# Cosine weights of four states on VectorE alone, Pool folding in three steps, gathers spread, another order of the drain

## The chip, the cores and the metric

The kernel runs as one program on one core of a Trainium2 chip. The metric is the device time of one execution in microseconds; three runs were made.

## What is computed

A recommendation tower over 1024 tokens. Two encoders (real and imaginary) turn the input into four states of 512 complex values for each token; attention over the four states, with 8 heads, follows; then the interference of the states, a measurement, and a small network. The interference is what the change is about:

```
R = attn_r @ int_Wr[n] - attn_i @ int_Wi[n]        # for each state n of 4
I = attn_r @ int_Wi[n] + attn_i @ int_Wr[n]
f = cos(angle between state i and state j) * strength[i, j]
sup_r = sum over i, j of f * R_j ;  sup_i = the same with I_j
sup   = sup / norm(sup)
mr, mi = sup times meas_Mr, meas_Mi ; amp = sqrt(mr^2 + mi^2)
out   = gelu(layernorm(amp @ post_W.T + post_b)) ; then three layers of the top network
```

The strengths, 16 for each token, are gathered from four embedding tables by index. In the kernel the cosine is the product of unit vectors (state divided by its magnitude), and a state of length zero counts as one with cosine 1.

## The kernel before

Three phases come one after the other: the first layers and the second layers of the encoders, up to about 1600 us, and `phase_states`, in which all of the change lies. There every engine has its own in-order list of instructions, written out by hand; semaphores tie the lists together, and there is no planner. Matrix products are done as three fp32r products of high and low parts (`split3`, lines 50 to 52).

**Attention.** 16 blocks of 64 tokens (`BT`). For each block TensorE projects queries and keys (`project`), scores (`score`), makes values (`values`), and for the block before it turns the softmax weights (`t_turn`, bank `pm`), mixes (`mix`) and projects out (`project_out`). ACT copies the turned weights (`pt_evac`), makes the high part of the mix (`o_high`) and of the output (`t_high`); VectorE spreads the weights (`spread`) and makes the low parts (`o_low`, `t_low`). SP loads block b+1 (`load_s`) when values of block b are done, and stores the output (`store_a`). After the loop the last block is drained by lists written out for each engine, among which weight pieces of the next stage are split (`pieces`). `o_high` of a block writes the buffer that `project_out` of the block before it reads, so it waits for that (`wo_full`). Pool issues 32 gathers for all eight token tiles in one go as soon as the indices are there.

**Interference.** 8 tiles of 128 tokens; the loops of the engines run over t. For each tile:
- SP loads the turned attention output of state n into one of two buffers (`load`); ACT negates a part (`negate`).
- TensorE: `vectors(t, n)`, 48 matmuls into banks 2n and 2n+1, for n = 0 to 3. It waits until the unit vector of tile t-1 has read the banks.
- ACT: `squares` (into `mag` and `sqi`), and after the sum, `magnitude` (a flag for zero, and the square root); for states 2 and 3 also `seed`, a reciprocal square root that VectorE refines.
- Pool: `add_squares`, the sum of two squares; `cosine` of pair (0, 1), two products and an addition into `pc` (`HELPED`); and `fold` of the tile before: states 0, 1 are added to 2, 3 (line 865), then those two to the sum `sup` (line 869). Its order is sums 0, 1, 2, both folds of t-1, sum 3, cosine.
- VectorE: `units` (reciprocal and unit vector for states 0 and 1, lines 1357 and 1370), `refine` (lines 1361 and 1363), unit vectors 2 and 3, then the six pairs: product (line 1382), inner addition (1383), addition of the zero flags (1384), and weighings (1393) into `inv`; `rescale` (1405); and at the end `product` (line 1443), the states times their weights, which signals `weighed`.
- ACT: `begin`, the first weight of each state, after the pairs (0, j); `length` and `scale` for the tile before.

Unit vector n of tile t+1 writes into `cs`, which the fold of tile t reads, so it waits for `folded`.

**Tail.** The last tile is written out; between its pairs lie the first stages of a pipeline over 8 tiles (turn, measure, amplitude, post, top layers), in which TensorE has about 20 us of work for each tile.

Of the kernel before, what the change touches and what calls it, by code (L numbers as in the profile page):

```python
# [9 lines left out]
ACT = mybir.ActivationFunctionType  # L10
# [486 lines left out]
def phase_states(nc, g):  # L497
# [13 lines left out]
    HELPED = [(0, 1)]  # L511
    WEIGHED = {(0, 1): 0, (0, 2): 1, (0, 3): 1, (1, 2): 2, (1, 3): 2, (2, 3): 2}
    TAKES = sum(WEIGHED[p] for p in HELPED)
    STEPS = 2 + 1 + 6 + 2 * (6 - len(HELPED)) + 3 + sum(WEIGHED.values()) - TAKES
    W_MR, W_MI, W_POST, W_T1, W_T2 = 0, KD, 2 * KD, 3 * KD, 4 * KD
    with s.ctx:
# [48 lines left out]
        pc = s.sb("pc", [P, 2, W])  # L565
# [69 lines left out]
        helped = s.sem("helped")  # L635
        taken = s.sem("taken")
# [87 lines left out]
        def p_of(i, j):  # L724
            return pc[:, 0, :] if (i, j) in HELPED else tt[:, 0, :]

        @block.sync
        def _(sp):
# [126 lines left out]
        @block.gpsimd  # L855
        def _(pool):
            def add_squares(t, n):
                pool.wait_ge(squared, t * 8 + (2 * n + 2))
                pool.tensor_tensor(sqi[:, n % 2, :], mag[:, n, :], sqi[:, n % 2, :], ALU.add).then_inc(summed, 1)

            def fold(t, i):

                if i == 0:
                    pool.wait_ge(weighed, t + 1)
                    pool.tensor_tensor(cs[:, :, 2:4, :], cs[:, :, 0:2, :], cs[:, :, 2:4, :], ALU.add).then_inc(folded, 1)
                else:
                    pool.wait_ge(folded, t * 2 + 1)
                    pool.wait_ge(stored, t * 16)
                    pool.tensor_tensor(sup[:, :, :], cs[:, :, 2, :], cs[:, :, 3, :], ALU.add).then_inc(folded, 1)

            def cosine(t, i, j):
                x = HELPED.index((i, j))
                pool.wait_ge(unit, done_units(t, j))

                if (i, j) == (0, 1):
                    if not zeroth(t):
                        if TAKES:
                            pool.wait_ge(taken, t * TAKES)
                        pool.wait_ge(w_begun, t * N)
                elif (i, j) == (0, 2):  # L880
                    pool.wait_ge(w_begun, t * N + 2)
                else:
                    pool.wait_ge(taken, t * TAKES + 1)
                    pool.wait_ge(w_begun, t * N + 3)
                for part in range(2):
                    pool.tensor_tensor(pc[:, part, :], cs[:, part, i, :], cs[:, part, j, :], ALU.mult).then_inc(helped, 1)
                pool.wait_ge(helped, t * (3 * len(HELPED)) + (3 * x + 2))
                pool.tensor_tensor(pc[:, 0, :], pc[:, 0, :], pc[:, 1, :], ALU.add).then_inc(helped, 1)

            def body(t, first):  # L890
                add_squares(t, 0)
                add_squares(t, 1)
                add_squares(t, 2)
                if not first:
                    fold(t - 1, 0)
                    fold(t - 1, 1)
                add_squares(t, 3)
                for i, j in HELPED:
                    cosine(t, i, j)
# [9 lines left out]
            body(0, True)  # L909
            body(1, False)  # L910
            with pool.Fori(2, TT) as t:
                body(t, False)
            fold(LAST, 0)
            fold(LAST, 1)

        @block.scalar
        def _(act):
# [104 lines left out]
            def squares(t, n):  # L1022
                act.wait_ge(multiplied, t * 8 + (2 * n + 2))
                if not zeroth(t):
                    act.wait_ge(rescaled, t * 3 - (2 - min(n, 2)))
                act.activation(mag[:, n, :], g.ps[:, 2 * n, :], ACT.Square).then_inc(squared, 1)
                if n >= 2:
                    act.wait_ge(mag_done, t * N + (n - 1))
# [4 lines left out]
            def magnitude(t, n):  # L1033
                act.wait_ge(summed, t * N + (n + 1))
                act.activation(zero[:, n, :], sqi[:, n % 2, :], ACT.Relu, scale=-1.0 / LEAST, bias=k01[:, 1:2])
                act.activation(mag[:, n, :], sqi[:, n % 2, :], ACT.Sqrt, bias=k01[:, 0:1]).then_inc(mag_done, 1)

            def seed(t):
                act.wait_ge(mag_done, t * N + N)
# [18 lines left out]
            def length(t):  # L1058
                act.wait_ge(folded, t * 2 + 2)
# [13 lines left out]
            def body(t, first):  # L1073
                squares(t, 0)
                magnitude(t, 0)
                negate(t, 3)
                squares(t, 1)
                magnitude(t, 1)
# [74 lines left out]
            t_high(LAST_B - 1, 3)  # L1153
            o_high(LAST_B, 1)
            pt_evac(LAST_B, 2)
            o_high(LAST_B, 2)
            pt_evac(LAST_B, 3)
# [19 lines left out]
            magnitude(t, 0)  # L1177
            negate(t, 3)
            squares(t, 1)
            magnitude(t, 1)  # L1180
            pieces(2 * NP, 2 * NP + KD)
            squares(t, 2)
            magnitude(t, 2)
# [3 lines left out]
            magnitude(t, 3)  # L1187
# [36 lines left out]
        def _(dve):  # L1224
# [118 lines left out]
            class Tile:  # L1343
                def __init__(self, t, first):
                    self.t, self.first, self.done, self.takes = t, first, 0, 0
# [7 lines left out]
                def invert(self, n):  # L1353
                    dve.wait_ge(mag_done, self.t * N + (n + 1))
# [3 lines left out]

                def refine(self):
                    dve.wait_ge(seeded, self.t + 1)  # L1360
                    self.link(dve.scalar_tensor_tensor(out=tt[:, :, :], in0=mag[:, 2:4, :], scalar=-1.0, in1=sqi[:, :, :],
                                                       op0=ALU.mult, op1=ALU.mult))
                    dve.scalar_tensor_tensor(out=inv[:, 2:4, :], in0=tt[:, :, :], scalar=2.0, in1=sqi[:, :, :],
# [3 lines left out]
                def unit_vector(self, n):  # L1367
                    if not self.first and n % 2 == 0:
                        dve.wait_ge(folded, self.t * 2 - (1 - n // 2))
# [3 lines left out]
                def pair(self, i, j):  # L1373
                    t, p = self.t, p_of(i, j)
                    self.link(dve.tensor_tensor(zz[:, :], zero[:, i, :], zero[:, j, :], ALU.add))
                    if (i, j) in HELPED:
                        dve.wait_ge(helped, t * (3 * len(HELPED)) + 3 * (HELPED.index((i, j)) + 1))
                    else:
                        dve.wait_ge(unit, done_units(t, j))
                        if (i, j) != (0, 2):  # L1380
                            dve.wait_ge(w_begun, t * N + (3 if i == 0 else 4))
                        self.link(dve.tensor_tensor(tt[:, :, :], cs[:, :, i, :], cs[:, :, j, :], ALU.mult))  # L1382
                        self.link(dve.tensor_tensor(p, p, tt[:, 1, :], ALU.add))  # L1383
# [7 lines left out]
                def weigh(self, i, j, a, b):  # L1391
                    dve.wait_ge(st_in, self.t + 1)
                    ins = dve.scalar_tensor_tensor(out=inv[:, b, :], in0=p_of(i, j),  # L1393
                                                   scalar=st[:, a * N + b:a * N + b + 1],
                                                   in1=inv[:, b, :], op0=ALU.mult, op1=ALU.add)
                    if (i, j) in HELPED:
                        ins.then_inc(taken, 1)
                        self.takes += 1
                        dve.wait_ge(taken, self.t * TAKES + self.takes)
                    else:  # L1400
                        self.link(ins)
# [39 lines left out]
                def product(self):  # L1441
# [3 lines left out]
                    assert self.done == STEPS and self.takes == TAKES  # L1445

            def body(t, first):
                tile = Tile(t, first)
                tile.units()
# [100 lines left out]
            sup_low(0)  # L1550
            tile.refine()
            tile.unit_vector(2)
            tile.unit_vector(3)
            tile.pair(0, 1)
# [37 lines left out]
        def _(pe):  # L1592
# [124 lines left out]
            project_out(LAST_B - 1, 2)  # L1717
            mix(LAST_B, 0)
            t_turn(LAST_B, 1)
# [236 lines left out]
```

## Time and profile before

| what | value |
|---|---|
| three runs | 3201.33, 3205.56, 3205.1 us; median 3205.1 |
| profiled execution | 3230.8 us, span 3229.1 us |
| TensorE busy | 3002.5 us (93%) |
| VectorE busy | 1566.5 us (49%) |
| ACT busy | 1118.1 us (35%) |
| Pool busy | 311.4 us (10%) |

The busy shares are means over stages of very different kind. In most of the first half of the span VectorE is busy for two tenths or less; in the interference stage, from about 2615 to 3060 us, for about eight. The profiled execution is one execution; the medians come from runs without a profile.

### The profile page before, as it was taken

The page shows a single profiled execution, that of the slowest core. Times are in us where ns is not written, and L with a number is a line of the kernel's source. Part 1 is how long each engine was busy: PE and PEld are TensorE (multiplying, and loading weights), DVE is VectorE, ACT ScalarE, POOL GpSimd, SP SyncE. Part 2 cuts the span into 40 slices and gives each one's busy share as a digit, 9 for nine tenths or more (in the row PEclk, how much of TensorE's full clock was granted, in tenths as well). Part 3 has the DMA queues.
Part 4 walks back from the last instruction along what each step waited for, and adds up shares of the span by engine and source line. Part 5 has one row for each costly group of instructions (what it writes and reads, how often), then busy time and mean ns, then how long its engine had stood idle before and what let it go on. Part 6 is the DMA issues. An engine that isn't in the chain of part 4 may idle for free. (4 is left out here: it accounts for less than half of the span.)

```text
span 3229.1 us, 43945 instructions
## 1 busy us (share of the span) xinstructions
PE 3002.5 (93%) x15808; PEld 2578.3 (80%) x15808; DVE 1566.5 (49%) x2779; ACT 1118.1 (35%) x1889; POOL 311.4 (10%) x289
## 2 busy tenths in 40 slices
PE   7999999999699999999759999999999989898798
PEld 6888888888588877888658999999999977676686
DVE  3222222221621216111156766767667658888873
ACT  3111111110421115111135555545545555454454
POOL 1000000000111101011130000000000003324200
PEclk9999999999899999999979999999999999999899
DMA  5222222221533325233332232231231374444410
GB/s 193 75 71 75 75 71 75 73 64 38 179 118 101 97 66 169 76 97 101 109 101 66 53 91 65 65 91 52 77 79 52 98 176 90 93 91 84 117 62 11
DMA packets 364352, 285.48 MB, mean 88 GB/s; under 512 B 280192, under 2 KB 280320, under 8 KB 364160
## 3 DMA queue, kind: packets, MB, share of 16 engines
q1 hardware_dynamic: 341632, 206.97, 24.0%
q0 software_dynamic: 22656, 77.67, 6.9%
q8 instruction: 38, 0.62, 0.1%
q14 instruction: 26, 0.21, 0.0%
HBM read 194.40 MB, written 90.18 MB: 88 GB/s over the span
## 5 line engine op out<-in xcount | busy, mean ns | idle before, releaser
L50 PE MATMUL banks<-a_whi,a_xhi 128*128 128x512 f32 x1152 | 450.1, 391 | 24.2 <-DVE a_wlo L179 17.7
L52 PE MATMUL banks<-a_whi,a_xlo 128*128 128x512 f32 x1152 | 449.0, 390 | 0.0
L51 PE MATMUL banks<-a_wlo,a_xhi 128*128 128x512 f32 x1152 | 448.9, 390 | 0.0
L50 PE MATMUL banks<-b_ghi,b_whi 128*128 128x512 f32 x1024 | 401.9, 392 | 10.0 <-DVE b_slo L389 8.8
L52 PE MATMUL banks<-b_ghi,b_wlo 128*128 128x512 f32 x1024 | 398.9, 390 | 0.0
L51 PE MATMUL banks<-b_glo,b_whi 128*128 128x512 f32 x1024 | 398.8, 389 | 0.0
L179 DVE TENSOR_TENSOR a_wlo<-a_wraw,a_whi 128x512 fp32r<-128x512 f32 x144 | 99.6, 691 | 577.3 <-ACT a_whi L165 577.3
L50 PE MATMUL banks<-t_sx,s_whi 128*128 128x256 f32 x1024 | 293.3, 286 | 58.4 <-DVE s_wlo L1309 24.1
L165 ACT ACTIVATE a_whi<-a_wraw 128x512 fp32r<-128x512 f32 x144 | 91.3, 634 | 667.2 <-PE banks L52 628.4
L374 DVE TENSOR_TENSOR b_wlo<-b_wraw,b_whi 128x512 fp32r<-128x512 f32 x128 | 88.2, 690 | 445.0 <-ACT b_whi L326 444.8
L52 PE MATMUL banks<-t_sx,s_wlo 128*128 128x256 f32 x1024 | 290.0, 283 | 0.0
L51 PE MATMUL banks<-t_sx,s_whi 128*128 128x256 f32 x1024 | 289.7, 283 | 0.0
L50 PEld LDWEIGHTS banks<-a_whi,a_xhi 128*128 128x128 f32 x1152 | 216.8, 188 | 72.2 <-issue 17.7
L1231 DVE TENSOR_SCALAR t_ks<-banks,cols 64x256 f32<-64x256 f32 x512 | 236.3, 481 | 63.3 <-PE banks L52 56.1
L52 PEld LDWEIGHTS banks<-a_whi,a_xlo 128*128 128x128 f32 x1152 | 216.7, 188 | 45.2
L51 PEld LDWEIGHTS banks<-a_wlo,a_xhi 128*128 128x128 f32 x1152 | 216.8, 188 | 44.9
L50 PE MATMUL banks<-s_whi,s_axng 128*128 128x512 f32 x512 | 209.2, 409 | 36.9 <-DVE s_cs L1370 34.0
L50 PEld LDWEIGHTS banks<-t_sx,s_whi 128*128 128x128 f32 x1024 | 195.8, 191 | 59.8 <-DVE s_wlo L1309 24.8
L326 ACT ACTIVATE b_whi<-b_wraw 128x512 fp32r<-128x512 f32 x128 | 80.5, 631 | 458.1 <-PE banks L52 457.3
L50 PEld LDWEIGHTS banks<-b_ghi,b_whi 128*128 128x128 f32 x1024 | 192.7, 188 | 54.9 <-DVE b_slo L389 13.3
L52 PEld LDWEIGHTS banks<-b_ghi,b_wlo 128*128 128x128 f32 x1024 | 192.4, 188 | 40.2
L51 PEld LDWEIGHTS banks<-b_glo,b_whi 128*128 128x128 f32 x1024 | 192.7, 188 | 39.2
(159 smaller groups left out, 5641.2 us busy)
## 6 DMA issues: line engine op xcount, KB each, us to landing
a_wraw<-w_first SPq DMA_DIRECT2D x144, 256.0 KB, 2.6
b_wraw<-w_second SPq DMA_DIRECT2D x128, 256.0 KB, 2.6
t_sx<-s_scr SPq DMA_DIRECT2D x64, 512.0 KB, 4.6
a_scr<-t_at SPq DMA_DIRECT2D x256, 128.0 KB, 2.1
s_axng<-a_scr SPq DMA_DIRECT2D x64, 512.0 KB, 6.0
s_wraw<-w_pieces SPq DMA_DIRECT2D x82, 256.0 KB, 4.6
h_scr<-a_hst POOLq DMA_DIRECT2D x72, 256.0 KB, 2.7
b_hl<-h_scr POOLq DMA_DIRECT2D x16, 1024.0 KB, 5.9
```

What stands on the lines that cost most here:

```text
L50: mm(out, ahi, bhi, start=first, stop=False)
L51: mm(out, ahi, blo, start=False, stop=False)
L52: return mm(out, alo, bhi, start=False, stop=last)
L165: act.activation(whi[:, k % SPL, :], wraw[:, k % RAW, :], ACT.Copy).then_inc(w_hi, 1)
L179: dve.tensor_tensor(wlo[:, k % SPL, :], wraw[:, k % RAW, :], whi[:, k % SPL, :].bitcast(F32), ALU.subtract).then_inc(w_split, 1)
L326: act.activation(whi[:, j % SPL, :, :].rearrange("p a n -> p (a n)"), wraw[:, j % RAW, :], ACT.Copy).then_inc(w_hi, 1)
L374: dve.tensor_tensor(wlo[:, j % SPL, :, :].rearrange("p a n -> p (a n)"), wraw[:, j % RAW, :], whi[:, j % SPL, :, :].bitcast(F32).rearrange ...
L1231: ins = dve.tensor_scalar(ks[half(at_half), m % 2, h, part, :], b_k[half(h), m % 2, e * C:(e + 1) * C], bcol(M_K + e, m, half(h)), float(s ...
```

## The change

- **Pool** no longer adds squares and no longer makes a cosine. It only folds, in three steps: state 0 to 2, state 1 to 3, and then those two to `sup`. A unit vector waits for the step that reads its state.
- **VectorE** adds the squares: those of states 2 and 3 in one instruction over 1024 elements (`add_23`, between unit vector 0 and reciprocal 1), those of states 0 and 1 of the next tile (`add_squares`) after pairs (1,2) and (2,3). It makes pair (0,1) whole, which now comes before `refine`.
- **ACT** squares into a buffer `sqr` of its own instead of `mag`, and takes the magnitudes of states 2 and 3 in one go. It no longer has to wait for `rescaled` before it squares, but before it takes a magnitude.
- **Gathers**: those of tile t wait for `projected` of block t+2, so that four are issued in each of the blocks 2 to 9.
- **Drain of the last block**: TensorE turns the weights of m+1 before it mixes m; ACT's `pt_evac` and VectorE's `spread` move ahead of `o_high` and `o_low`.
- **SP**: `load(0, 2)` moves ahead of the last eight weight pieces of the stage.
- **Last tile**: `pair(0, 1)` moves ahead of `refine` there too, behind `pieces` and `sup_low(0)`.

```diff
@@ sync
             for i in range(NP + 4 * KD, NP + 6 * KD):
                 piece(i)
+            load(0, 2)
             sp.wait_ge(wo_full, LAST_B * 4 + 4)
             for i in range(NP + 6 * KD, 2 * NP):
                 piece(i)
-            load(0, 2)
             load(0, 3)
@@ gpsimd
-            def add_squares(t, n):
-                pool.wait_ge(squared, t * 8 + (2 * n + 2))
-                pool.tensor_tensor(sqi[:, n % 2, :], mag[:, n, :], sqi[:, n % 2, :], ALU.add).then_inc(summed, 1)
...
+            def fold(t):
+                pool.wait_ge(weighed, t + 1)
+                for n in range(2):
+                    pool.tensor_tensor(cs[:, :, n + 2, :], cs[:, :, n, :], cs[:, :, n + 2, :], ALU.add).then_inc(folded, 1)
+                pool.wait_ge(folded, t * 3 + 2)
+                pool.wait_ge(stored, t * 16)
+                pool.tensor_tensor(sup[:, :, :], cs[:, :, 2, :], cs[:, :, 3, :], ALU.add).then_inc(folded, 1)
             for t in range(TT):
+                pool.wait_ge(projected, (t + 2) * 8 + 5)
                 for f, tbl in enumerate((g.tbl_0, g.tbl_1, g.tbl_2, g.tbl_3)):
...
@@ scalar
             def squares(t, n):
                 act.wait_ge(multiplied, t * 8 + (2 * n + 2))
-                if not zeroth(t):
-                    act.wait_ge(rescaled, t * 3 - (2 - min(n, 2)))
-                act.activation(mag[:, n, :], g.ps[:, 2 * n, :], ACT.Square).then_inc(squared, 1)
...
+                act.activation(sqr[:, n % 2, :], g.ps[:, 2 * n, :], ACT.Square).then_inc(squared, 1)
...
                 squares(t, 2)
-                magnitude(t, 2)
                 squares(t, 3)
-                magnitude(t, 3)
+                magnitude(t, 2, 4)
                 seed(t)
@@ scalar, drain of the last block
+            pt_evac(LAST_B, 1)
             o_high(LAST_B, 0)
-            pt_evac(LAST_B, 1)
...
@@ vector
+                def add_23(self):
+                    dve.wait_ge(squared, self.t * 8 + 8)
+                    dve.tensor_tensor(sqi[:, :, :], sqr[:, :, :], sqi[:, :, :], ALU.add).then_inc(summed, 1)
...
                 def units(self):
                     self.invert(0)
                     self.unit_vector(0)
+                    self.add_23()
                     self.invert(1)
                     self.unit_vector(1)
...
                 tile.units()
+                tile.pair(0, 1)
                 tile.refine()
                 tile.unit_vector(2)
                 tile.unit_vector(3)
-                tile.pair(0, 1)
                 tile.pairs_02()
...
                 tile.pairs_12()
+                add_squares(t + 1, 0)
                 tile.pairs_13()
                 tile.pairs_23()
+                add_squares(t + 1, 1)
                 tile.product()
@@ vector, drain of the last block
+            spread(LAST_B, 2)
             o_low(LAST_B, 0)
-            spread(LAST_B, 2)
             pieces(NP + 2, NP + 4)
             t_low(LAST_B - 1, 3)
+            spread(LAST_B, 3)
             o_low(LAST_B, 1)
-            spread(LAST_B, 3)
@@ tensor, drain of the last block
             project_out(LAST_B - 1, 2)
+            t_turn(LAST_B, 1)
             mix(LAST_B, 0)
-            t_turn(LAST_B, 1)
             project_out(LAST_B - 1, 3)
+            t_turn(LAST_B, 2)
             mix(LAST_B, 1)
-            t_turn(LAST_B, 2)
+            t_turn(LAST_B, 3)
             mix(LAST_B, 2)
-            t_turn(LAST_B, 3)
             mix(LAST_B, 3)
```

## Rows read from the trace of the kernel before

**Rows 1.** Windows: stretch, length, busy us of each engine, TensorE's granted clock, DMA.

```profile
2655.00:2707.00 52.00, 52.00 (x224) 41.84 (x223) 36.95 (x40) 24.44 (x37) 9.57 (x7) 1.00 0.51 100
2812.00:2865.00 53.00, 47.52 (x196) 37.84 (x196) 46.97 (x44) 26.74 (x41) 17.26 (x9) 0.94 0.44 89
```

**Rows 2.** Waits, 2330 to 3229 us: waiting <- releaser, us, times, longest.

```profile
PE banks L50 <- DVE s_cs L1370: 34.0, 6, 6.1
...
DVE s_tt L1361 <- ACT s_sqi L1040: 24.8, 7, 13.9
```

**Rows 3.** Timeline of TensorE and ACT: start, duration, instruction, idle before.

```profile
2641.38 0.50 PE L50 MATMUL banks<-s_whi,s_axng 128*128 128x512 f32 x1 [2.92 <-DMA s_axng<-a_scr]
...
2820.49 0.79 PE L50 MATMUL banks<-s_whi,s_axng 128*128 128x512 f32 x1 [5.49 <-DVE s_cs L1370]
...
2825.62 1.16 ACT L1040 ACTIVATE s_sqi<-s_sqi,s_k 128x1024 f32<-128x1024 f32 x1
...
2863.17 1.16 ACT L1019 ACTIVATE s_axng<-s_axng 128x512 fp32r<-128x512 f32 x2 [4.26 <-DMA s_axng<-a_scr]
```

**Rows 4.** Timeline of VectorE, interference stage.

```profile
2703.52 4.43 DVE L1443 TENSOR_TENSOR s_cs<-s_cs,s_inv 128x4096 f32<-128x4096 f32 x1
...
2809.14 4.42 DVE L1443 TENSOR_TENSOR s_cs<-s_cs,s_inv 128x4096 f32<-128x4096 f32 x1
...
2819.21 1.23 DVE L1370 TENSOR_TENSOR s_cs<-banks,s_inv 128x1024 f32<-128x1024 f32 x1 [2.19 <-POOL s_cs L865]
...
2826.81 1.86 DVE L1361 SCALAR_TENSOR_TENSOR s_tt<-s_mag,s_sqi 128x1024 f32<-128x1024 f32 x1 [1.85 <-ACT s_sqi L1040]
...
2835.04 1.23 DVE L1382 TENSOR_TENSOR s_tt<-s_cs 128x1024 f32<-128x1024 f32 x1
...
2846.86 2.45 DVE L1393 SCALAR_TENSOR_TENSOR s_inv<-s_tt,s_st,s_inv 128x512 f32<-128x512 f32 x2
...
2856.42 1.67 DVE L1383 TENSOR_TENSOR s_tt<-s_tt 128x512 f32<-128x512 f32 x1
...
3020.46 4.42 DVE L1443 TENSOR_TENSOR s_cs<-s_cs,s_inv 128x4096 f32<-128x4096 f32 x1
```

**Rows 5.** Two lines of VectorE: count, shortest/median/longest ns.

```profile
L1361 DVE SCALAR_TENSOR_TENSOR s_tt<-s_mag,s_sqi x8: 1210/1844/2018, 2671.0 to 3046.1; 128x1024 f32<-128x1024 f32 x8
...
L1363 DVE SCALAR_TENSOR_TENSOR s_inv<-s_tt,s_sqi x8: 1225/2198/2203, 2672.2 to 3047.3; 128x1024 f32<-128x1024 f32 x8
```

**Rows 6.** Timeline of Pool, the two folds of a tile.

```profile
2814.68 4.50 POOL L865 TENSOR_TENSOR s_cs<-s_cs 128x2048 f32<-128x2048 f32 x1
2819.34 2.36 POOL L869 TENSOR_TENSOR s_sup<-s_cs 128x1024 f32<-128x1024 f32 x1 [0.16 <-POOL s_cs L865]
```

**Rows 7.** Timeline of TensorE and VectorE in the drain of the last block.

```profile
2589.87 1.16 PE L1663 MATMUL banks<-t_ptl,t_v 128*128 128x128 f32 x8 [2.71 <-ACT t_ptl L939]
...
2603.76 2.00 DVE L1289 SCALAR_TENSOR_TENSOR t_olo<-banks,cols,t_ohi 64x256 fp32r<-64x256 f32 x4 [3.44 <-ACT t_ohi L948]
```

**Rows 8.** Timeline of VectorE: last instruction of sup_low(1).

```profile
3060.60 0.68 DVE L1470 SCALAR_TENSOR_TENSOR s_wlo<-banks,s_whi 128x512 fp32r<-128x512 f32 x1
```

**Rows 9.** Timelines around the gathers (first and last of 32), and DMA issues, 1640 to 1664.

```profile
1649.14 1.02 POOL L906 DMA_INDIRECT s_emb<-tbl,s_ids  x1 [45.48 <-DMA s_ids<-ids]
...
1662.24 0.40 PE L52 MATMUL banks<-s_whi,t_sx 128*128 128x512 f32 x1
1673.45 0.55 PE L50 MATMUL banks<-t_sx,s_whi 128*128 128x256 f32 x1 [10.81 <-issue]
...
1688.10 0.95 POOL L906 DMA_INDIRECT s_emb<-tbl,s_ids  x1 [0.30 <-issue]
...
1694.31 0.60 ACT L956 ACTIVATE t_v<-banks 128x512 f32<-128x512 f32 x1 [21.12 <-remote]
...
1699.80 0.58 PE L50 MATMUL banks<-t_sx,s_whi 128*128 128x256 f32 x1 [23.45 <-DMA t_sx<-s_scr]
...
t_sx<-s_scr SPq DMA_DIRECT2D x2, 512.0 KB
```

More of the change, by code:

```diff
@@ L509, in phase_states @@
     FLOOR = 2e-38
-    HELPED = [(0, 1)]
     WEIGHED = {(0, 1): 0, (0, 2): 1, (0, 3): 1, (1, 2): 2, (1, 3): 2, (2, 3): 2}
-    TAKES = sum(WEIGHED[p] for p in HELPED)
-    STEPS = 2 + 1 + 6 + 2 * (6 - len(HELPED)) + 3 + sum(WEIGHED.values()) - TAKES
+    STEPS = 2 + 1 + 6 + 2 * 6 + 3 + sum(WEIGHED.values())
     W_MR, W_MI, W_POST, W_T1, W_T2 = 0, KD, 2 * KD, 3 * KD, 4 * KD
@@ L724, in p_of @@
         def p_of(i, j):
-            return pc[:, 0, :] if (i, j) in HELPED else tt[:, 0, :]
+            return tt[:, 0, :]
         @block.sync
@@ L856, in _ @@
         def _(pool):
-            def add_squares(t, n):
-                pool.wait_ge(squared, t * 8 + (2 * n + 2))
-                pool.tensor_tensor(sqi[:, n % 2, :], mag[:, n, :], sqi[:, n % 2, :], ALU.add).then_inc(summed, 1)
[L861 to L875, printed above, removed]
-                    if not zeroth(t):
[L877 to L899, printed above, removed]
+            def fold(t):
[5 more added lines that the diff above has]
+                pool.tensor_tensor(sup[:, :, :], cs[:, :, 2, :], cs[:, :, 3, :], ALU.add).then_inc(folded, 1)
@@ L908, in _ @@
                         in_offset=bass.IndirectOffsetOnAxis(ap=ids[:, t, f:f + 1].bitcast(U32), axis=0)).then_inc(emb_in, 16)
[L909 to L914, printed above, removed]
+            fold(0)
+            with pool.Fori(1, TT) as t:
+                fold(t)
         @block.scalar
@@ L1344, in __init__ @@
                 def __init__(self, t, first):
-                    self.t, self.first, self.done, self.takes = t, first, 0, 0
+                    self.t, self.first, self.done = t, first, 0
                 def link(self, ins):
@@ L1367, in unit_vector @@
                 def unit_vector(self, n):
-                    if not self.first and n % 2 == 0:
-                        dve.wait_ge(folded, self.t * 2 - (1 - n // 2))
+                    if not self.first and n < 3:
+                        dve.wait_ge(folded, self.t * 3 - (2 - n))
                     dve.tensor_tensor(cs[:, :, n, :], g.ps[:, 2 * n:2 * n + 2, :],
@@ L1375, in pair @@
                     self.link(dve.tensor_tensor(zz[:, :], zero[:, i, :], zero[:, j, :], ALU.add))
[L1376 to L1383, printed above, removed]
+                    dve.wait_ge(unit, done_units(t, j))
+                    if (i, j) != (0, 1):
+                        dve.wait_ge(w_begun, t * N + (j if i == 0 else 4))
+                    elif not self.first:
+                        dve.wait_ge(w_begun, t * N)
+                    self.link(dve.tensor_tensor(tt[:, :, :], cs[:, :, i, :], cs[:, :, j, :], ALU.mult))
+                    self.link(dve.tensor_tensor(p, p, tt[:, 1, :], ALU.add))
                     ins = dve.tensor_tensor(p, p, zz[:, :], ALU.add)
@@ L1392, in weigh @@
                     dve.wait_ge(st_in, self.t + 1)
[L1393 to L1401, printed above, removed]
+                    self.link(dve.scalar_tensor_tensor(out=inv[:, b, :], in0=p_of(i, j),
+                                                       scalar=st[:, a * N + b:a * N + b + 1],
+                                                       in1=inv[:, b, :], op0=ALU.mult, op1=ALU.add))
                 def rescale(self, n0, n1):
@@ L1444, in product, with add_squares @@
                                       ALU.mult).then_inc(weighed, 1)
-                    assert self.done == STEPS and self.takes == TAKES
+                    assert self.done == STEPS
+            def add_squares(t, n):
+                dve.wait_ge(squared, t * 8 + (2 * n + 2))
+                dve.tensor_tensor(sqi[:, n, :], sqr[:, n, :], sqi[:, n, :], ALU.add).then_inc(summed, 1)
             def body(t, first):
                 tile = Tile(t, first)
+                if first:
+                    add_squares(t, 0)
+                    add_squares(t, 1)
                 tile.units()
+                tile.pair(0, 1)
                 tile.refine()
@@ L1550, in _ @@
             sup_low(0)
+            tile.pair(0, 1)
             tile.refine()
@@ L1553, in _ @@
             tile.unit_vector(3)
-            tile.pair(0, 1)
             tile.pairs_02()
```

44 lines of the change are left out of this document (22 added, 22 removed).

## The prediction

> **What bounds the kernel.** The windows come first, because the run has stages with different limits [rows 1]. While nothing stops it, TensorE issues 224 matmuls in 52 us, one per 0.232 us, so the 192 matmuls of a tile of the interference stage need 44.6 us. In the repeating part of that stage TensorE is busy for 47.5 of 53 us, at a granted clock of 0.94, and VectorE for 46.97 of 53. In the tail TensorE is busy all the time from 3093 us on, so what shifts the time before that shifts the end.
>
> The waits say who is late [rows 2]: TensorE waits for VectorE's unit vector of state 0, six times some 5.7 us, because that vector frees the banks that the next tile's first products need. One of these waits stands in [rows 3]; the first matmul behind it takes 0.79 us and the clock is back later, which the 0.94 shows too. So look at what makes VectorE late [rows 4]. Its `product` of tile 0 starts at 2703.52 and that of tile 6 at 3020.46: six periods of 52.8 us. The list has little free time. Inside a period it waits 2.19 us for Pool's fold and 1.85 us for ACT's seed (the waits give 24.8 us for seven, 13.9 of it in tile 0), and some 0.5 us in scraps. The rest is work, part of it slow: the two refine instructions take 1.84 and 2.20 us where their shortest take 1.21 and 1.23 [rows 5]; the pair of weighings at 2846.86 takes 2.45 where others take 1.54; the add at 2856.42 takes 1.67 where others take 0.69. In each case a Pool `tensor_tensor` runs beside it. That is 0.63 + 0.97 + 0.92 + 0.98 = 3.5 us a period. VectorE's in-order list is the bound, and TensorE, with 44.6 us, follows it.
>
> **Interference, steady tiles.** What goes: the fold wait. Pool did the fourth addition of squares, the folds and the cosine behind one another; its 4.50 us fold [rows 6] began 1.1 us after the product and released unit vector 0. Now Pool has only folds, begins right behind `weighed`, and its first step, half of the 4.50, is over after 2.4 us, while the reciprocal takes 3.35. So this wait costs nothing. If Pool began 1.1 us later it would still be hidden, by about nothing. The seed wait goes too: the sum over states 2 and 3 comes early, at `add_23`, and behind it stand reciprocal 1 (3.4), unit vector 1 (1.2) and pair (0,1) (3.2), 7.8 us in front of `refine`; ACT needs about 5 us there (the row at 2825.62 in [rows 3] has one pass over 1024 elements at 1.16; three such and a table load). The collisions with Pool's additions and cosine go, as Pool no longer does them: 3.5 us.
>
> What comes to VectorE: `add_23` over 1024 elements, priced by the product of pair (0,2) at 1.23 [rows 4], 1.25 with its gap; two `add_squares` over 512, 0.65 each; the product of pair (0,1), 1.26, and its inner addition, 0.73 with the gap. Sum 4.54. I add 0.3 for the third `begin` of ACT, which now comes closer to pair (1,2): ACT reaches it behind a negation whose load lands some 7.5 us after TensorE frees the buffer. The new period is 52.8 - 4.5 - 3.5 + 4.54 + 0.3 = 49.65 us, still more than TensorE's 44.6, or 46.4 with the slow restart. The gain is 3.2 us a period, 19 us over six.
>
> Does anything else get late? TensorE's n = 3 product of tile t+1 ends 46.5 us after unit vector 0; ACT's two squares of it need 1.2 us. `add_23` of tile t+1 is asked for about 49.6 us after the former unit vector: 1.9 us of slack. Behind `add_23` stand reciprocal 1 and all pairs, so this slack matters. ACT's negation for the next tile stands ahead of those squares and waits for its load: in [rows 3] the row at 2863.17 shows it 4.26 us idle for it. It lands in time by the same 7.5 us, some 3 us before the squares are wanted.
>
> The three-step fold makes Pool's reads end 8 us after the product. `add_23` falls into this. It is issued 4.6 us behind the product's end, and Pool's second step ends at about 4.75. The third waits on a semaphore (0.16 us in [rows 6]: from the end at 2819.18 to 2819.34), so VectorE should go in between and lose 0.1 us. The ends are 0 and 2.4 us, a whole step (2.36 for 1024 elements). I take 0.1, inside the 0.3.
>
> That an instruction is held back for a whole one of the other engine is what these rows show: 1.67 - 0.69 us is nearly the length of Pool's addition. The Trainium skill (SBUF — State Buffer, Who interferes with whom) states it as an exclusive lock for VectorE instructions with two SBUF inputs, held for the full instruction, and won by the one that issues first. Had that rule given Pool the third step first, the sum would lose 6 x 2.3 = 14 us; by the order in the row it loses under 1. This hangs on 0.2 us of timing, so it is a rival below.
>
> **Tile 0 and its start.** In tile 0 `add_23` has to wait for TensorE's last product, and reciprocal 1, unit vector 1 and pair (0,1), which before were done in that wait, now stand behind it. Before, pair (0,2) began 12.9 us after that product (2676.95 against 2664.1); now it is 1.2 + 1.25 + 3.4 + 1.2 + 3.2 + 2.5 + 2.3 = about 15.0, so 2.1 later. Two adds more, 1.3, and two collisions less, 2.0: a loss of 1.4 us.
>
> Against it: SP issues `load(0, 2)` ahead of the last eight weight pieces. TensorE sat 2.92 us for this load [rows 3]. It will be there, but ACT negates it only behind all pieces, and these land up to 3 us later than now, as 1 MB goes ahead of them. I take half of the stall back at least, 1.9 us; 0 to 2.9 are the ends.
>
> The drain order puts pt_evac(1) ahead of o_high(0), which waits until 2587.2 for the last output projection. TensorE no longer sits 2.71 us for it [rows 7], and the last o_low, at 2603.76 before, comes some 3.4 us earlier by the same durations in the new order. But TensorE then runs its 18 matmuls behind o_low(2), at the slow clock, where before they were already done: 1.6 us are left (0 to 3.4). Together 3.5 - 1.4 = 2.1 us of gain.
>
> **Tail.** The last tile has `pair(0, 1)` behind the eight pieces and sup_low(0). The latter ends 0.7 us sooner after the product, for want of waits; but sup_low(1) comes behind 2.0 us more pair work, partly covered by seed and fold waits that are gone. It ended at 3061.28 [rows 8], 36.4 us after the product of tile 6; laid out by the same durations it ends 36.7 after it. From there the list is the old one: a loss of 0.3.
>
> **Gathers.** They are 32, one each 1.25 us, from 1649.14 to 1689 [rows 9]. Just there TensorE stops for 10.81 and 23.45 us. Its last matmul of the values starts at 1662.24, but ACT evacuates them only at 1694.31, and SP issues the next load then. Without delay the load would land at about 1667.2, TensorE would go on there, not at 1699.80: 32.6 us. Spread over eight blocks, four gathers (5 us) a block, with Pool otherwise idle, they hide behind the block's own work, and this stall goes, in the profile.
>
> Is it there without a profile? The profiled execution took 3230.8 us (span 3229.1), the median is 3205.1: 25.7 less. Take the stall away and 3198.2 is left. And in that stretch two t_sx loads have no landing time in their row, as if records were lost. I read most of the stall as the recording's. The bounds are 0 and 32.6; the 6.9 us between 3205.1 and 3198.2 may be a real rest of it. I take half, 3.5.
>
> **Sum.** 19.0 + 2.1 - 0.3 + 3.5 = 24.3 us, so 3205.1 - 24.3 = 3180.8, say 3181. Against the profiled execution: 3230.8 - 20.8 - 32.6 = about 3177.
>
> **Rivals.** (a) Gathers stall the unprofiled run as well: all 32.6 us come back, 3205.1 - 20.8 - 32.6 = 3152. For it: ACT and SP really start late. Against: the 25.7 us. (b) Pool's third step goes first and holds `add_23` each tile: 14 us less, 3195. Against: the 0.16 us gap. (c) The loop is bound elsewhere, by ACT's chain for the third `begin` or by the loads, and VectorE's freed 3.2 us turn into waits: the edit of the loop does nothing, 3180.8 + 19 = 3200. For it: slacks under 2 us. (d) Slower: `add_23`, in the midst of VectorE's list, waits for ACT's squares of n = 3, queued behind a negation that waits for a load. From 1.9 us of lateness on every us costs six; at 1.9 + 3.2 = 5.1 the gain is used up, and at 7 us it is 3205.1 - 5.3 + 6 x 1.9 = 3211. For it: ACT was idle up to 4.26 us for such loads. Against: the load would have to land 10 us late.
>
> **Chances.** Forecast 0.58 (its own range 3174 to 3189), (a) 0.16, (b) 0.10, (c) 0.09, (d) 0.07. What this kernel's measurement can tell from no change is about 0.2%, 6.4 us. (a) and (b) are faster; (c) is split between faster and same. Faster 0.86, same 0.07, slower 0.07. The range from 3150 to 3196 holds the forecast, (a) and (b).
>
> **What would show it.** `product` every 49 to 50 us; unit vector 0 without a wait for Pool; `add_23` of 1.2 us (b: up to 3.6); refine instructions at 1.2 us; no wait of `add_23` for squares except in tile 0; TensorE waiting some 3 to 5 us a tile, still for unit vector 0; no stop between 1662 and 1700. It is wrong if VectorE waits for ACT in each period, if a Pool step stands in front of `add_23`, or if the profiled and unprofiled times of the new kernel differ by as much as now.

## Result, and the profile after

| kernel | executions | median us | ratio to before, 95% |
|---|---|---|---|
| before, first comparison | 4 | 3205.11 | |
| after, first comparison | 4 | 3179.22 | 0.9928 [0.9916, 0.9940] |
| before, second comparison | 21 | 3201.12 | |
| after, second comparison | 5 | 3179.14 | 0.9931 [0.9917, 0.9944] |

The change makes the kernel 22 to 26 us faster; 3181 was forecast, within 3150 to 3196. For every kernel but before, the profiled execution is one of those counted. The changed kernel took the same on both occasions, the kernel before did not: 3205.1 in the first comparison, 3200.6, 3201.1 and 3201.9 in three later ones. The smaller difference, 22.0 us, rests on more executions, and the accounts below are made against it. The profiled execution of after took 3182.7 us (span 3181.0), 3.5 more than the median, where that of before took 25.7 more. Busy are TensorE 2999.9 us, VectorE 1573.5, ACT 1111.3 and Pool 232.9.

The timeline of VectorE in the changed kernel: start, duration, engine, line, operation, and in brackets the idle time ahead of it. The rows are the product of tile 0, `add_23` of tile 0, then the period that begins with the product of tile 1, and the product of tile 6. They answer to [rows 4].

```profile
2633.91 1.23 DVE L1319 TENSOR_TENSOR s_sqi<-s_sqr,s_sqi 128x1024 f32<-128x1024 f32 x1 [9.26 <-ACT s_sqi L987]
...
2673.23 4.42 DVE L1399 TENSOR_TENSOR s_cs<-s_cs,s_inv 128x4096 f32<-128x4096 f32 x1
...
2723.56 4.42 DVE L1399 TENSOR_TENSOR s_cs<-s_cs,s_inv 128x4096 f32<-128x4096 f32 x1
2728.08 3.35 DVE L1315 RECIPROCAL s_inv<-s_mag 128x512 f32<-128x512 f32 x1
2731.56 1.23 DVE L1332 TENSOR_TENSOR s_cs<-banks,s_inv 128x1024 f32<-128x1024 f32 x1
2732.70 1.22 DVE L1319 TENSOR_TENSOR s_sqi<-s_sqr,s_sqi 128x1024 f32<-128x1024 f32 x1
...
2738.44 0.42 DVE L1337 TENSOR_TENSOR s_zz<-s_zero 128x512 bf16<-128x512 bf16 x1
2739.06 1.23 DVE L1343 TENSOR_TENSOR s_tt<-s_cs 128x1024 f32<-128x1024 f32 x1 [0.20 <-DVE s_zz L1337]
...
2741.87 1.23 DVE L1323 SCALAR_TENSOR_TENSOR s_sqr<-s_mag,s_sqi 128x1024 f32<-128x1024 f32 x1
2743.13 1.23 DVE L1325 SCALAR_TENSOR_TENSOR s_inv<-s_sqr,s_sqi 128x1024 f32<-128x1024 f32 x1
2744.39 2.35 DVE L1332 TENSOR_TENSOR s_cs<-banks,s_inv 128x1024 f32<-128x1024 f32 x2
2746.66 0.41 DVE L1337 TENSOR_TENSOR s_zz<-s_zero 128x512 bf16<-128x512 bf16 x1
2747.64 1.22 DVE L1343 TENSOR_TENSOR s_tt<-s_cs 128x1024 f32<-128x1024 f32 x1 [0.56 <-DVE s_zz L1337]
...
2972.72 4.42 DVE L1399 TENSOR_TENSOR s_cs<-s_cs,s_inv 128x4096 f32<-128x4096 f32 x1
```

From 2673.23 to 2972.72 are six periods of 49.92 us, where [rows 4] have 52.8. Unit vector 0 (2731.56) has no wait for Pool any more, refine (2741.87) none for ACT's seed, and the two refine instructions take 1.23 us each, not 1.84 and 2.20. `add_23` waits for ACT's squares in tile 0 alone.

One wait for ACT is left, in two of the six periods: the product of pair (1, 2) waits for ACT's third `begin`, 1.95 us in the first and 0.88 us in the fourth. The second of them in the timeline, and both in the view of waits, 2673 to 2973 us:

```profile
2856.62 1.23 DVE L1343 TENSOR_TENSOR s_tt<-s_cs 128x1024 f32<-128x1024 f32 x1 [0.88 <-ACT s_inv L1015]
```

```profile
DVE s_tt L1343 <- ACT s_inv L1015: 2.8, 2, 1.9
```

Pool in the same period (also the timeline), which answers to [rows 6], and TensorE's wait for unit vector 0 (the view of waits: us in all, times, longest), which answers to [rows 2]:

```profile
2728.06 4.70 POOL L856 TENSOR_TENSOR s_cs<-s_cs 128x1024 f32<-128x1024 f32 x2 [42.33 <-DVE s_cs L1399]
2732.92 3.24 POOL L859 TENSOR_TENSOR s_sup<-s_cs 128x1024 f32<-128x1024 f32 x1 [0.17 <-POOL s_cs L856]
```

```profile
PE banks L50 <- DVE s_cs L1332: 19.4, 6, 4.9
```

Pool's second step ends at 2732.76; `add_23` has gone in at 2732.70, and the third step, 0.16 us behind the second, takes 3.24 us instead of 2.36. So it is Pool that is held, for 0.9 us, and nobody waits for that. TensorE still waits for unit vector 0 six times, now 3.2 us on average instead of 5.7. VectorE's list is still the bound.

### The profile page after: what moved, and what is told of

Read it like the earlier page. It is cut to its first block and busy times, and to the rows that moved or that the text cites. A ratio compares the mean times of both kernels' runs of the same rounds, so it can differ in the third digit from the quotient of the medians.

```text
span 3181.0 us, 43948 instructions
## 1 busy us (share of the span) xinstructions
PE 2999.9 (94%) x15808; PEld 2577.4 (81%) x15808; DVE 1573.5 (49%) x2819; ACT 1111.3 (35%) x1873; POOL 232.9 (7%) x241
## 3 DMA queue, kind: packets, MB, share of 16 engines
q1 hardware_dynamic: 341632, 206.97, 24.3%
```

## Experiments

"The mark" below is the start of VectorE's product of a tile; products of tiles 0 and 6 are six periods apart. Each comparison has its own executions of the kernel before.

**The gathers alone, and where they stand.** The first kernel is before with one line added:

```diff
             for t in range(TT):
+                pool.wait_ge(projected, (t + 2) * 8 + 5)
                 for f, tbl in enumerate((g.tbl_0, g.tbl_1, g.tbl_2, g.tbl_3)):
```

> The kernel before, with the gathers spread over eight blocks and nothing else changed. Theory (the stop near 1662 us is mostly the recording's, a rest of some 7 us is real): 3198 us unprofiled, and the profiled execution within 1 us of the unprofiled ones, with no stop of TensorE over 5 us between 1662 and 1700. Rival 1, the stop is the recording's alone: unprofiled 3205, profiled near 3198 to 3205. Rival 2, the whole stop is in the unprofiled run too: 3172 unprofiled.

Measured: 3201.54 (11 executions), before 3200.62 (21), ratio 1.0005 [0.9996, 1.0014]; the span of the profiled one is 3197.5. By that interval, spreading the gathers gains at most 1.3 us. The stop was not in the unprofiled time, and my real rest of some 7 us isn't there.

The second is after without that line, the third is before with the 32 gathers together but behind `projected` of block 2, the fourth is before itself, profiled again.

> The changed kernel with the 32 gathers in one go again. Theory: 3179.2 + 7 = 3186 unprofiled, profiled some 25 us above that, TensorE stopped near 1662 to 1700 us as in the kernel before. Rival 1 (the recording's alone): 3179. Rival 2 (wholly real): 3212.

Measured: 3180.37, before 3200.62; ratio 0.9932 [0.9918, 0.9945]. The profiled execution took 3180.37 too, with no stop. That is rival 1, and not the 3186 of the theory.

> The kernel before, its 32 gathers in one go but held back until the queries and keys of block 2 are projected, about 100 us later. If what costs time is 32 gathers issued together, wherever they stand: unprofiled as before, 3205, and a stop of TensorE of 20 to 35 us in the profile, now near 1750 us. If it is that they fall together with the start of the attention stage (its first loads, whose queue is Pool's neighbour): 3198 as with the gathers spread, and no stop.

Measured: 3200.36 (11 executions), ratio 1.0000 [0.9991, 1.0010], and no stop in the profile. Neither reading holds: the time is that of before, and there is no stop.

> The kernel before, unchanged, profiled once more. Theory (the stop of TensorE between 1662 and 1700 us was an event of that one recording, as neither kernel with bunched gathers shows it again): span near 3199, no stop over 5 us there. Rival (it comes with the bunched gathers under this kernel's own timing): the stop of some 30 us again, span near 3230.

Measured: 3204.96, span 3203.2, no stop. Windows of the same 70 us, with busy time and count of PE, PEld, DVE, ACT and POOL, then PE's granted clock: first of before as in the recording that the prediction used, then of the new recording of the same kernel, then of after with bunched gathers.

```profile
1640.00:1710.00 70.00, 35.63 (x202) 32.03 (x202) 27.53 (x56) 18.91 (x35) 30.46 (x32) 0.73 0.23 61
```

```profile
1640.00:1710.00 70.00, 65.34 (x428) 60.34 (x427) 56.05 (x116) 37.87 (x73) 30.47 (x32) 0.98 0.24 62
```

```profile
1640.00:1710.00 70.00, 66.22 (x431) 60.99 (x431) 56.03 (x116) 38.20 (x73) 30.60 (x32) 0.98 0.25 72
```

All three have the same 32 instructions on Pool, first at 1649 to 1652 us, busy for the same 30.5 us. Only the first has TensorE at 35.63 us. The stop of [rows 9] was an event of one recording. It wasn't caused by the gathers in any way that repeats: four other recordings with 32 gathers together (before again, before with them later, after with them bunched, and the loop alone, below) don't have it. What it was stays open.

**The loop alone.** After with the gathers, the drain and the place of `load(0, 2)` of before, so that only the lists of the interference stage differ from before:

```diff
-            load(0, 2)
             sp.wait_ge(wo_full, LAST_B * 4 + 4)
             for i in range(NP + 6 * KD, 2 * NP):
                 piece(i)
+            load(0, 2)
             load(0, 3)
```

(and the drain lists of ACT, VectorE and TensorE, and Pool's line, turned back likewise)

> The changed kernel with the drain order, the place of load(0, 2) and the gathers of before: the edit of Pool's, ACT's and VectorE's lists in the interference stage alone. Theory: six periods of 49.9 us as in the changed kernel, 17.5 us less than before, and tile 0 and the tail together near nothing: 3205.1 - 17.5 = 3188 unprofiled, profiled some 25 us more. Rival, the earlier start or the spread gathers carry a part of the loop's gain: 3193 or more.

Measured: 3180.33, before 3200.62: 20.3 us less, ratio 0.9938 [0.9924, 0.9951]. The rival falls: the edit of the lists carries nearly the whole effect. It is more than the 17 us of the six periods (49.87 us each here, 52.7 in before), since the last tile gains too: from the product of tile 6 to that of tile 7 are 79.1 us, where before has 82.5. The next rows say why. First the timeline of before with spread gathers, in its last tile: the products of tiles 6 and 7, and between them VectorE's weight pieces and Pool beside them:

```profile
2987.36 4.42 DVE L1444 TENSOR_TENSOR s_cs<-s_cs,s_inv 128x4096 f32<-128x4096 f32 x1
...
3003.17 8.10 DVE L1310 TENSOR_TENSOR s_wlo<-s_wraw,s_whi 128x512 fp32r<-128x512 f32 x8
...
3003.33 3.31 POOL L886 TENSOR_TENSOR s_pc<-s_cs 128x512 f32<-128x512 f32 x2 [2.19 <-DVE s_cs L1371]
3006.72 1.59 POOL L888 TENSOR_TENSOR s_pc<-s_pc 128x512 f32<-128x512 f32 x1
...
3069.88 4.41 DVE L1444 TENSOR_TENSOR s_cs<-s_cs,s_inv 128x4096 f32<-128x4096 f32 x1
```

And after, where the product of tile 6 starts at 2972.72:

```profile
2987.41 4.90 DVE L1267 TENSOR_TENSOR s_wlo<-s_wraw,s_whi 128x512 fp32r<-128x512 f32 x8
...
3051.81 4.42 DVE L1399 TENSOR_TENSOR s_cs<-s_cs,s_inv 128x4096 f32<-128x4096 f32 x1
```

The eight pieces have two inputs in SBUF and ran beside Pool's cosine; without it they take 3.2 us less, of the 3.4 by which this stretch is shorter. The prediction looked for such collisions in the repeated period, not here.

**Is it really the side-by-side work?** After, in which Pool multiplies two magnitudes by one behind unit vector 1; the values stay what they are:

```diff
+            def idle(t):
+                pool.wait_ge(unit, done_units(t, 1))
+                for n in range(2):
+                    pool.tensor_tensor(mag[:, n, :], mag[:, n, :], k01[:, 1:2].to_broadcast([P, W]), ALU.mult).then_inc(idled, 1)
+                pool.wait_ge(idled, t * 3 + 2)
+                pool.tensor_tensor(mag[:, 0, :], mag[:, 0, :], k01[:, 1:2].to_broadcast([P, W]), ALU.mult).then_inc(idled, 1)
...
                 def rescale(self, n0, n1):
+                    dve.wait_ge(idled, self.t * 3 + 3)
```

> The changed kernel, in which Pool multiplies the magnitudes of states 0 and 1 by one, in three instructions over 512 elements a tile, right behind unit vector 1: work that nobody needs, where the cosine of the pair stood before. Theory (VectorE instructions that meet a Pool tensor_tensor are held back by about its length): 2 to 3.5 us a period, in the last tile slower weight pieces, some 20 us in all: 3200. Rival (the gain of the loop came from the removed waits alone; side by side they cost nothing): 3180.

Measured: 3193.23 (11 executions), after 3179.14 beside it: 14.1 us more. The timeline, VectorE's pair (0, 1) and its pieces in the last tile, and Pool:

```profile
2741.27 1.78 DVE L1353 TENSOR_TENSOR s_tt<-s_cs 128x1024 f32<-128x1024 f32 x1 [0.20 <-DVE s_zz L1347]
2743.09 1.41 DVE L1354 TENSOR_TENSOR s_tt<-s_tt 128x512 f32<-128x512 f32 x1
2744.53 1.42 DVE L1355 TENSOR_TENSOR s_tt<-s_tt,s_zz 128x512 f32<-128x512 f32 x1
...
2997.99 7.42 DVE L1277 TENSOR_TENSOR s_wlo<-s_wraw,s_whi 128x512 fp32r<-128x512 f32 x8
...
2740.82 3.13 POOL L874 TENSOR_TENSOR s_mag<-s_mag,s_k 128x512 f32<-128x512 f32 x2 [2.44 <-DVE s_cs L1342]
2744.03 1.37 POOL L876 TENSOR_TENSOR s_mag<-s_mag,s_k 128x512 f32<-128x512 f32 x1
```

Three instructions whose results change nothing (`rescale` waits for them, but starts without idle time) cost VectorE 0.55 + 0.72 + 0.73 = 2.0 us in the pair, of which 1.9 show in the period (51.5 against 49.6), and the pieces take 7.42 us, 2.5 more. Six times 1.9 and 2.5 are 13.9 us. The mechanism holds, a little under the size that was expected: 1.9 us a period where 2 to 3.5 were, 14 us and not 20. The rival falls.

**The changed kernel again**, beside the last one and the next two.

> The changed kernel once more, beside the kernel before on the same chip. Both earlier calls agree on nothing but the sign: 25.9 us less where the kernel before took 3205.1, some 20 less for two variants where it took 3200.6. If the difference lies in the chip or the day: 20 us less than the kernel before here. If it is what the spread gathers add to the rest of the change: 25 us less here too.

Measured: 3179.14 (5 executions), before 3201.12 (21); 22.0 us less. It is the same time as in the first comparison, so the difference of 4 us between the two comparisons is one of the kernel before. The 25 us that the spread gathers might have given aren't there.

**Two steps or three.**

```diff
-                for n in range(2):
-                    pool.tensor_tensor(cs[:, :, n + 2, :], cs[:, :, n, :], cs[:, :, n + 2, :], ALU.add).then_inc(folded, 1)
+                pool.tensor_tensor(cs[:, :, 2:4, :], cs[:, :, 0:2, :], cs[:, :, 2:4, :], ALU.add).then_inc(folded, 2)
```

> The changed kernel with Pool's fold in two steps instead of three, states 0 and 1 to 2 and 3 in one instruction of 4.5 us. Theory: unit vector 0 waits 1.2 us for it, and the last step now begins before add_23 is issued and holds it back 1.3 us more: 2.5 us a tile, seven tiles, 17 us more than the changed kernel. Rival (a Pool instruction holds nothing back, only the semaphore counts): 1.2 us a tile, 8 us more.

Measured: 3194.21 (11 executions), 15.1 us more than after; the theory had 17, the rival 8. Timeline of VectorE and Pool:

```profile
2731.95 1.23 DVE L1331 TENSOR_TENSOR s_cs<-banks,s_inv 128x1024 f32<-128x1024 f32 x1 [1.28 <-POOL s_cs L855]
2733.09 2.43 DVE L1318 TENSOR_TENSOR s_sqi<-s_sqr,s_sqi 128x1024 f32<-128x1024 f32 x1
...
2727.36 4.56 POOL L855 TENSOR_TENSOR s_cs<-s_cs 128x2048 f32<-128x2048 f32 x1 [44.44 <-DVE s_cs L1398]
2732.09 2.35 POOL L858 TENSOR_TENSOR s_sup<-s_cs 128x1024 f32<-128x1024 f32 x1 [0.17 <-POOL s_cs L855]
```

This is rival (b) of the prediction made real. Now Pool's last step starts first, 1.0 us ahead of `add_23`, runs its 2.35 us undisturbed, and `add_23` takes 2.43. In after it is the other way round: `add_23` 1.22, the step 3.24. Both times the one that started second is longer by nearly what the first had left: 1.21 us of 1.35 here, 0.88 of 1.00 in after. The Trainium skill (SBUF — State Buffer, Who interferes with whom) says that issue order, not the shape, decides who is blocked; these two traces agree.

**The place of `add_23`.** Behind unit vector 1 instead of unit vector 0, in every tile:

```diff
                     self.unit_vector(0)
-                    self.add_23()
                     self.invert(1)
                     self.unit_vector(1)
+                    self.add_23()
```

> The changed kernel with add_23 behind unit vector 1 instead of behind unit vector 0, in every tile. ACT's chain from the sum to the seed is 4.5 to 4.7 us long; then only pair (0, 1), 3.2 us, covers it. Theory (the seed wait was bought off by the place of add_23): refine waits 1.3 to 1.5 us a tile, but add_23 no longer holds Pool's third step; 1.4 x 7 = 10 us more than the changed kernel, 3189. Rival (the period is set by what TensorE or ACT deliver, and VectorE has slack): 3179.

Measured: 3183.08, before 3201.86, ratio 0.9941 [0.9928, 0.9955]; 18.8 us less than before, where after has 22.0.

```profile
2789.80 1.23 DVE L1323 SCALAR_TENSOR_TENSOR s_sqr<-s_mag,s_sqi 128x1024 f32<-128x1024 f32 x1 [1.51 <-ACT s_sqi L1000]
...
2779.42 2.37 POOL L859 TENSOR_TENSOR s_sup<-s_cs 128x1024 f32<-128x1024 f32 x1 [0.16 <-POOL s_cs L856]
```

The seed wait is back, 1.51 us, and the period is 51.0, 1.4 more than the 49.6 of after, 8 us over six. The total is only 3 to 4 us more, where the theory had 10, because tile 0 gains: there reciprocal 1 and unit vector 1 now lie in the wait for TensorE (from Pool's memset to the product of tile 0 are 1064.7 us, where after has 1068). That led to the next one. Pool's last step beside a reciprocal, which has one input, takes 2.37: it isn't held.

**Tile 0 in another order.**

```diff
                     self.unit_vector(0)
-                    self.add_23()
+                    if not self.first:
+                        self.add_23()
...
                 tile.pair(0, 1)
+                if first:
+                    tile.add_23()
                 tile.refine()
```

> The changed kernel, in which VectorE's add_23 of tile 0 alone stands behind pair (0, 1), so that reciprocal 1, unit vector 1 and the pair are done while TensorE's last product of the tile is awaited. Theory: refine then waits for ACT's seed only, which ended at 2639.8 where refine began at 2642.7: 2.8 us less than the changed kernel. Rival, what tile 0 gains is given back in a wait of TensorE or in the last stretch: no difference.

Measured: 3175.70, after 3179.14 beside it: 3.4 us less, five executions each, whose ranges overlap by 2.3 us; ratio to before 0.9918 [0.9905, 0.9932]. VectorE's timeline in tile 0:

```profile
2633.70 1.22 DVE L1319 TENSOR_TENSOR s_sqi<-s_sqr,s_sqi 128x1024 f32<-128x1024 f32 x1 [1.76 <-ACT s_sqi L987]
2639.65 1.23 DVE L1323 SCALAR_TENSOR_TENSOR s_sqr<-s_mag,s_sqi 128x1024 f32<-128x1024 f32 x1 [4.72 <-ACT s_sqi L1000]
```

The wait of 9.26 us is 1.76, the seed wait of 4.72 comes in its place, and refine begins 19.9 us after reciprocal 0, where after has 22.7.

**The drain alone.** After with the old order in the drain of the last block, `load(0, 2)` kept ahead.

```diff
-            t_turn(LAST_B, 1)
             mix(LAST_B, 0)
+            t_turn(LAST_B, 1)
```

(and so on, as in the diff of the change, turned back)

> The changed kernel with the drain of the last block in the old order; load(0, 2) stays ahead of the pieces. Theory: the last o_low comes 2 to 3 us later and product(0) 1 us: 3180 where the changed kernel takes 3179. Rival (the prediction's 1.6 us for the drain, all of it lasting to the end): 3180.8 or more.

Measured: 3178.36 (3176.93 to 3183.38), ratio 0.9931 [0.9918, 0.9945], the same as after. The order of the drain can't be told from nothing here: the theory of 1 us and the rival of 1.6 us or more are both within the spread of these five executions.

**A scrap in each pair.** Besides tile 0's new order, the product no longer waits for the sum of zero flags ahead of it, which it doesn't read:

```diff
-                    self.link(dve.tensor_tensor(zz[:, :], zero[:, i, :], zero[:, j, :], ALU.add))
+                    dve.tensor_tensor(zz[:, :], zero[:, i, :], zero[:, j, :], ALU.add).then_inc(chain, 1)
+                    self.done += 1
```

> The changed kernel with add_23 of tile 0 behind pair (0, 1), and with each pair's product no longer waiting for the addition of the zero flags in front of it, which it doesn't read (waits of 0.20 us in pair (0, 1) and 0.12 us of start delay in each of six pairs). Theory (VectorE's in-order list sets the period, so every scrap counts): 0.5 to 0.9 us a tile, 4 to 6 us less than the one with add_23 alone: 3170 to 3172. Rival (pairs (0, 2), (0, 3) and (1, 2) wait for ACT's first weights anyway): 1 to 2 us less, 3174.

Measured: 3166.77 (4 executions), before 3201.86: 35.1 us less, ratio 0.9889 [0.9874, 0.9904]. It beats both kernels. Timeline, the zero flags and product of pairs (0, 1) and (0, 2):

```profile
2779.29 0.41 DVE L1337 TENSOR_TENSOR s_zz<-s_zero 128x512 bf16<-128x512 bf16 x1
2779.62 1.22 DVE L1344 TENSOR_TENSOR s_tt<-s_cs 128x1024 f32<-128x1024 f32 x1
...
2787.22 0.41 DVE L1337 TENSOR_TENSOR s_zz<-s_zero 128x512 bf16<-128x512 bf16 x1
2787.55 1.22 DVE L1344 TENSOR_TENSOR s_tt<-s_cs 128x1024 f32<-128x1024 f32 x1
```

From the flags to the product are 0.33 us both times; in after 0.62 and 0.98 (2738.44 to 2739.06, 2746.66 to 2747.64). The shortest periods are 48.15 instead of 49.63. Six times 1.5 and 0.7 in the last tile are 9.7 us; against the kernel with tile 0's new order alone the median is 8.9 us lower, in another comparison. Both are more than the 4 to 6 expected, and the rival falls: it wasn't ACT's first weight that these products waited for. Only pair (1, 2) still waits for ACT, 0.6 to 0.7 us in two of the six periods.

## Why the prediction was right, term by term

The likeliest case came true, and what was to show it is in the trace. Its terms did less well than their sum, and that the sum fits so closely is in part luck: two errors of about 3.5 us cancel. With the marks of four recordings of before-like lists in the loop (52.82, 52.63, 52.62, 52.74 us a period) and five of after-like ones (49.91, 49.91, 49.87, 49.67, 49.65):

| term | forecast us | measured us |
|---|---|---|
| loop, six periods | 19.0 | 17.4 (2.9 each) |
| tile 0, load, drain | 2.1 | 1.7 |
| tail | -0.3 | 3.1 |
| gathers | 3.5 | 0 |
| sum | 24.3 | 22.2 (the comparison: 22.0) |

**Loop.** Right, with its reasons. Three of the six periods of after are 49.63 or 49.64, against 49.65 forecast; the others are 49.87, 50.33 and 50.39. The last two hold the waits for ACT's third `begin`, 1.95 and 0.88 us. In that place the prediction has 0.3 us a period, with its reason: ACT reaches the `begin` behind a negation that waits for a load. The five recordings have 1.1 to 2.9 us of this wait in six periods, 0.36 a period in the mean; but it comes as one or two long waits and not in every tile. The work that VectorE took over costs 1.13 + 2 x 0.61 + 1.26 + 0.73 = 4.3 us from start to start, where 4.54 was forecast. Three of the gains were taken away again, one kernel each: the Pool fold wait (two steps instead of three: 1.28 us back, together with 1.2 for the order at `add_23`), the seed wait (1.51 back), the side-by-side work (1.9 of the 3.5 us back, by three Pool instructions where before had seven outside its folds). What is missing to 19.0 are 0.15 us a period, by which the five are over 49.65 in the mean, and 0.12, by which the first recording of before was over the mean of four. Rival (c), a loop that gains nothing, is refuted; rival (d) too: ACT's squares of n = 3 ended at 2731.3, 1.4 us ahead of `add_23` (forecast 1.9).

**Tile 0, load, drain.** From Pool's memset at the start of the phase to the product of tile 0, the three recordings of before's lists without a stop take 1068.5 to 1070.5, the loop alone 1069.4, the three of after and of after with bunched gathers 1066.1 to 1068.5. By the means tile 0 loses 0.2, not 1.4, and load and drain give 1.9, not 3.5. Single recordings differ by 1 to 2 us there, so this term is only known to be small.

**Tail.** The step that failed: "sup_low(1) comes behind 2.0 us more pair work, partly covered". It counted Pool's collisions in the repeated period only. In the last tile they hit the eight weight pieces as well, 3.2 us. In the trace of after sup_low(1) ends 32.9 us after the end of the product of tile 6, where 36.7 was forecast. From the product of tile 6 to the end, before needs 208.6 to 210.5 (mean 209.8 of four), after-like kernels 205.2 to 208.3 (mean 206.7 of five). All of this gain lies ahead of the product of tile 7 (82.5 us against 79.1); from there to the end it is 127.2 and 127.6 us in the mean.

**Gathers.** The step that failed: "the 6.9 us between 3205.1 and 3198.2 may be a real rest of it. I take half". The 3198.2 is one execution less its stop, and single executions of before reach from 3197.7 to 3206.7; 6.9 us lie within that. That the stop did not belong to the unprofiled runs was right, and was rightly read from the 25.7 us between them and the profiled one. That the gathers cause it in a recording, and that spreading them takes it away there, is not borne out: four recordings with the gathers together have no stop. Errors of -3.5 and +3.4 us cancelled. The 4 us by which the kernel before was slower in the first comparison are not explained; nothing in these runs puts them down to the change.

## What to carry to other kernels

When an in-order VectorE list is the bound, look at what runs beside it on Pool: three Pool `tensor_tensor` for which no engine stood idle cost 1.9 us a period, and taking such work over onto the full engine was a gain. Then look for waits on instructions whose result isn't read, and count collisions in the written-out first and last tile as well as in the loop. Before a gap in one recording is priced, record the kernel a second time.

## What the runs showed of the hardware

**A wait for the instruction just ahead cost 0.1 to 0.65 us here.** The product of pair (0, 2) stood 0.56 us idle behind flags that had been issued 0.98 us before and took 0.41; without the wait it begins 0.33 us after them, before they are over. In that run its other waits, for its unit vector and ACT's weight, were met by then, as that beginning shows. From flags to product, start to start, after has 0.62, 0.75 (once 0.98), 0.61, 0.54, 0.45 and 0.45 us for the six pairs of a tile from tile 2 on, and 0.45 for the first three in tile 1, ACT's late weight left out; without the wait it is 0.32 to 0.34 for all of them. The smallest case, pair (1, 3) in the timeline of after:

```profile
2761.59 0.42 DVE L1337 TENSOR_TENSOR s_zz<-s_zero 128x512 bf16<-128x512 bf16 x1
2762.04 1.23 DVE L1343 TENSOR_TENSOR s_tt<-s_cs 128x1024 f32<-128x1024 f32 x1
```

Why the same wait costs five times as much in one pair as in another wasn't tried.

**The clock near the end of the run differs between executions.** The last stretch of loop-alone and of after with bunched gathers holds the same instructions at the same distances, up to a wait of 2.34 us for VectorE near the end. Then one goes on at the full clock and the other at half. The timeline and the windows (length, busy us and count of PE, PEld, DVE, ACT and POOL, then TensorE's granted clock), first of the loop alone:

```profile
3159.76 0.47 PE L50 MATMUL banks<-s_whi 128*128 128x512 f32 x1 [2.34 <-DVE s_wlo L1464]
...
3159.50:3165.50 6.00, 5.04 (x28) 4.17 (x28) 2.26 (x6) 0.05 (x1) 0.00 (x0) 1.00 0.01 3
```

and of after with bunched gathers:

```profile
3157.76 0.77 PE L50 MATMUL banks<-s_whi 128*128 128x512 f32 x1 [2.34 <-DVE s_wlo L1464]
...
3157.50:3163.50 6.00, 5.74 (x15) 4.62 (x16) 0.88 (x3) 0.00 (x0) 0.00 (x0) 0.50 0.00 0
```

28 matmuls in 6 us at a granted clock of 1.00 (2.4 GHz), 15 at 0.50 (1.2 GHz). From the product of tile 6 to the end the one takes 205.2 us, the other 207.9. That is 2.7 us which no edit made, as large as several terms of the sum. So 0.0 us between the medians of these two kernels, of five executions each, doesn't show that drain and load are worth nothing. TensorE had done the same before that in both, so what decides is not in these rows. Of the four recordings of before's lists one keeps the granted clock at 1.00 there, and of the five after-like ones two. The wait also shows that TensorE isn't busy to the end of the tail, as the prediction took it to be.
